# A decoder layer on one core: identity products in the front, an earlier first v, and the second gate and up ahead of P V

## What is computed

```python
x = x + attn(layernorm(x))            # sigmoid q, k; kv = k^T v per head; num/den; norm; gate; Wo; relu
x = x + xattn(layernorm(x), ctx)      # 16 heads of 64: softmax(q k^T / 8) v, then Wo + bo
x = x + ffn(layernorm(x))             # shared SwiGLU (256) + the SwiGLU of the expert that top-1 of 8 picks
```

## Time and profile before

| | us |
|---|---|
| median of 3 timed runs | 648.67 |
| lowest and highest | 648.15, 648.98 |
| the profiled execution | 643.3 |
| its span, first to last instruction | 641.6 |
| TensorE busy | 593.4 |
| VectorE busy | 428.0 |
| ScalarE busy | 424.9 |
| GpSimd busy | 310.7 |

### The profile page before, as it was taken

How to read it: one execution, slowest core, us unless ns; L and a number is a source line. 1 busy time by engine, 2 the same in 40 slices (tenths; PEclk the granted TensorE clock), 3 DMA queues, 4 the chain that set the end, 5 groups by cost and what they waited for, 6 DMA issues and landing times.

```text
span 641.6 us, 14968 instructions
## 1 busy us (share of the span) xinstructions
PE 593.4 (92%) x5231; PEld 514.1 (80%) x5231; DVE 428.0 (67%) x1185; ACT 424.9 (66%) x1512; POOL 310.7 (48%) x331
## 2 busy tenths in 40 slices
PE   3868999999999999999999999999999987999993
PEld 2767799889988998899989988998889876766661
DVE  3858665878685868586858685868564566376562
ACT  3538788777776787678677867786768764444551
POOL 3524644365336633663366336633652354147553
PEclk9969999999999999999999999999999998899997
DMA  7300000000010001000100000000000007325420
GB/s 161 98 18 13 17 2 2 13 18 2 2 30 18 17 3 30 18 18 2 30 18 17 1 15 17 17 2 2 17 18 1 2 27 227 115 72 157 144 74 8
DMA packets 24953, 23.49 MB, mean 37 GB/s; under 512 B 7007, under 2 KB 22497, under 8 KB 24880
## 3 DMA queue, kind: packets, MB, share of 16 engines
q1 hardware_dynamic: 20368, 14.91, 8.6%
q0 software_dynamic: 2784, 6.32, 2.7%
q10 hardware_dynamic: 1728, 1.32, 0.9%
HBM read 15.03 MB, written 7.95 MB: 36 GB/s over the span
## 4 chain that ended last, share of the span: by engine, by line
PE 70%; DVE 15%; ACT 7%; issue 3%; DMA 1%; POOL 1%; SPq 0%; DVEq 0%; POOLq 0%
PE bank L1128 9%; PE bank L1275 9%; PE bank L1243 8%; PE bank L1130 7%; PE bank L1129 7%; PE bank L1253 7%; PE bank L1264 5%; PE bank L1355 4%; ACT prob L1031 4%; PE bank L1224 2%; PE bank L1380 2%; PE bank L1135 2%; DVE stats L648 2%; DVE mneg L816 2%; ACT oT L1041 2%
## 5 line engine op out<-in xcount | busy, mean ns | idle before, releaser
L1031 ACT ACTIVATE prob<-bank,mneg 128x128 f32<-128x128 f32 x512 | 182.0, 376 | 80.1 <-DVE mneg L816 79.9
L560 POOL TENSOR_TENSOR prob<-prob,rden 128x512 f32<-128x512 f32 x128 | 130.7, 1041 | 107.1 <-DVE rden L823 106.8
L1031 ACT ACTIVATION_READ_ACCUMULATOR prob<-bank,mneg 128x1 f32 x512 | 109.8, 214 | 0.0
L1037 ACT COPY probT<-bank 128x512 f32<-128x512 f32 x128 | 76.8, 600 | 36.7 <-PE bank L1253 36.6
L816 DVE TENSOR_REDUCE mneg<-bank 128x4 f32<-128x512 f32 x128 | 80.3, 669 | 18.5 <-PE bank L1243 18.4
L1253 PE MATMUL bank<-ident,prob 128*128 128x128 f32 x512 | 78.4, 276 | 5.5 <-POOL prob L560 4.7
L499 POOL TENSOR_TENSOR rstd<-var_eps,neg_half 128x4 f32<-128x4 f32 x24 | 24.7, 1029 | 114.6 <-DVE var_eps L653 114.6
L1243 PE MATMUL bank<-kT,qT 64*128 64x128 f32 x1024 | 74.4, 285 | 2.9 <-issue 1.7
L1243 PEld LDWEIGHTS bank<-kT,qT 64*128 64x128 f32 x1024 | 62.2, 187 | 14.0 <-issue 11.4
L1253 PEld LDWEIGHTS bank<-ident,prob 128*128 128x128 f32 x512 | 60.6, 142 | 10.6 <-issue 6.2
L1264 PE MATMUL bank<-probT,V 128*64 128x128 f32 x1024 | 64.2, 279 | 0.0
(11 more groups left out here) (194 smaller groups left out, 1332.9 us busy)
## 6 DMA issues: line engine op xcount, KB each, us to landing
prob<-routed SPq DMA_DIRECT2D x39, 128.5 KB, 2.1
xin<-in_x_dram SPq DMA_DIRECT2D x8, 256.0 KB, 2.8
ctx_nat<-in_ctx_dram SPq DMA_DIRECT2D x8, 192.0 KB, 2.5
routed<-blank ACTq DMA_DIRECT2D x8, 128.5 KB
qT<-in_L_ffn_rt_gate_dram SPq DMA_DIRECT2D x1, 1024.0 KB, 5.9
qT<-in_L_ffn_rt_up_dram SPq DMA_DIRECT2D x1, 1024.0 KB, 11.1
out_dram<-probT,prob POOLq DMA_INDIRECT x39, 2.2
prob<-in_L_xattn_Wq_dram SPq DMA_DIRECT2D x1, 512.0 KB, 6.1
```

Of the source, the lines that this page charges most:

```text
L560: nc.gpsimd.tensor_tensor(view, view, spread(rden[:, m % 2, c * NC:(c + 1) * NC], 2, S), ALU.mult)\
L1031: last = nc.scalar.activation(prob[:, m % 2, p * S:(p + 1) * S], score_bank(m, c)[:, i * S:(i + 1) * S], ACT.Exp, bias=mneg[:, m % 2, p:p ...
L1037: nc.scalar.copy(probT[:, m % 2, c * 512:(c + 1) * 512], made(r1, ("T", m, c))[:])\
```

## The change

- The load of bq counts on a semaphore of its own. ScalarE's first casts wait for four loads, and the sigmoid of q for bq.
- TensorE multiplies the identity by itself 22 times at its start, as soon as the identity is there, and 8 times in slot (-4, 2) ahead of the turn of x1, into a bank of the scores that is unused then.
- Both halves of v of sequence 0 are made in slot (-4, 1), ahead of the last early piece of k, and emptied by ScalarE. They were made in (-1, 1) and (-1, 3) and emptied by VectorE. ScalarE's rounding of the cross-v weights goes from (-5, 3) to (-5, 2), VectorE's low part from (-4, 1) to (-5, 3), ahead of x1.
- The statistics of the second group of x go from (-5, 2) to behind those of x1, ahead of the normalisation of x1. GpSimd's rstd of them goes from (-5, 2) to (-4, 2).
- In the loop, "gate and up 1" is done ahead of P V in its slot, and "tanh 1" ahead of the copies of P V. VectorE's order stays.

```diff
--- before.py
+++ after.py
@@ -225,6 +225,7 @@
 
         w_in = sem("s1_weights_landed")
+        bq_in = sem("q_bias_landed")
         wx_in = [sem("cross_q_weights_landed"), sem("cross_k_weights_landed"), sem("cross_v_weights_landed")]
         wo_in = sem("output_weights_landed")
         xwo_in = sem("cross_output_weights_landed")
@@ -332,7 +333,7 @@
                  (NG - 2, "scatter 2"): (L6 + 2, 1), (NG - 2, "scatter 3"): (L6 + 2, 1),
                  (0, "turn context"): (-7, 2), (0, "context high"): (-7, 2), (0, "context low"): (-7, 2),
                  (0, "residual"): (-3, 0),
-                 (1, "stats of x"): (-5, 2), (1, "rstd of x"): (-5, 2), (1, "normalise x"): (-4, 3),
+                 (1, "stats of x"): None, (1, "rstd of x"): (-4, 2), (1, "normalise x"): (-4, 3),
                  (1, "turn x"): (-2, 3), (1, "copy x^T"): (-2, 3), (1, "x^T low"): (-2, 3),
                  (1, "project first pair"): (-1, 0), (1, "first pair"): (-1, 0),
                  (1, "project second pair"): (-1, 1), (1, "second pair"): (-1, 1)}
@@ -372,6 +373,12 @@
             pair = (n + 3) // 2 if n % 2 else (n + 2) // 2
             return early + [(part, pair, b)] * ((2 if part == "k" else 0) <= pair < B // 2)
+        def v_of(n, b):
+            if (n, b) == (-4, 1):
+                return [(0, 0), (0, 1)]
+            return [(n + 1, b // 2)] * (b % 2 and 0 < n + 1 < B)
         def qk_engine(part, pair, i):
             return "act" if i % 2 or (part == "k" and pair < 2) else "dve"
@@ -382,8 +389,8 @@
             for b in range(NC):
                 if live(n):
                     r1.add(("T", n, b), "act")
-                if b % 2 and live(n + 1):
-                    r1.add(("v", n + 1, b // 2), "dve")
+                for m, half in v_of(n, b):
+                    r1.add(("v", m, half), "dve" if m else "act")
                 for piece in qk_of(n, b):
                     r1.add(piece, qk_engine(*piece))
                 if b == 0 and live(n - 1):
@@ -391,12 +398,17 @@
                     r1.add(("PV", n - 1, 1), "act")
                 if b == 2 and live(n - 1):
                     r1.add(("out", n - 1), "dve")
+                for g, step in steps_at(PE_F, F_AT, n, b):
+                    if step == "gate and up 1":
+                        for u, engine in F_BANKS[step]:
+                            r2.add((g, u), engine)
                 for g, step in steps_at(PE_S1, S1_AT, n, b):
                     for u, engine in S1_BANKS[step]:
                         r2.add((g, u), engine)
                 for g, step in steps_at(PE_F, F_AT, n, b):
-                    for u, engine in F_BANKS[step]:
-                        r2.add((g, u), engine)
+                    if step != "gate and up 1":
+                        for u, engine in F_BANKS[step]:
+                            r2.add((g, u), engine)
         for step in itertools.chain.from_iterable(PE_TAIL.values()):
             for u, engine in F_BANKS[step]:
@@ -431,7 +443,7 @@
             sp.dma_start(rawkvh[:, D:2 * D], Wk).then_inc(w_in, 16)
             sp.dma_start(rawkvh[:, 2 * D:], Wv).then_inc(w_in, 16)
             sp.dma_start(rawq1, Wq).then_inc(w_in, 16)
-            sp.dma_start(bq_col[:], bq.rearrange("(p o) -> p o", o=1)).then_inc(w_in, 16)
+            sp.dma_start(bq_col[:], bq.rearrange("(p o) -> p o", o=1)).then_inc(bq_in, 16)
             load_ctx(0)
             sp.dma_start(rawk, XWk).then_inc(wx_in[0], 16)
             sp.dma_start(lnw_bc[:], bc(ln_w)).then_inc(wl_in, 16)
@@ -739,6 +751,8 @@
                     dve.wait_ge(x1_in, g + 1)
                     stats_of(2, x1)
                     if g == 0:
+                        s1(1, "stats of x")
                         normalise_first(x1n, x1, 2)
                 if step == "context low":
                     ps = made(r2, (g, 13))
@@ -915,8 +929,9 @@
                     if b % 2 == 0 and live(n + 1):
                         row_max(n + 1, b)
                         row_max(n + 1, b + 1)
-                    if b % 2 and live(n + 1):
-                        empty_v(n + 1, b // 2)
+                    for m, half in v_of(n, b):
+                        if m > 0:
+                            empty_v(m, half)
                     for piece in qk_of(n, b):
                         if qk_engine(*piece) == "dve":
                             empty_qk(*piece)
@@ -935,7 +950,7 @@
                         dve.wait_ge(wm_hi, 1)
                         nc.vector.tensor_tensor(sh_gu_lo[:], rawgu, sh_gu_hi[:].bitcast(F32), ALU.subtract)\
                             .then_inc(wm_lo, 1)
-                    if (n, b) == (FIRST + 3, 1):
+                    if (n, b) == (FIRST + 2, 3):
                         dve.wait_ge(w_hi, 3)
                         nc.vector.tensor_tensor(xwv_lo[:], rawv, xwv_hi[:].bitcast(F32), ALU.subtract)\
                             .then_inc(w_lo, 1)
@@ -1003,7 +1018,7 @@
                     nc.scalar.activation(hkv[:, :, D:2 * D], hkv[:, :, D:2 * D], ACT.Sigmoid).then_inc(k_sig, 1)
                     ps = made(r2, (g, 5))
                     if g == 0:
-                        act.wait_ge(w_in, 16 * 5)
+                        act.wait_ge(bq_in, 16)
                     nc.scalar.activation(qsT[:], ps[:], ACT.Sigmoid, bias=bq_col[:]).then_inc(r2.emptied["act"], 1)
                 if step == "copy gated^T":
                     nc.scalar.copy(gT[:], made(r2, (g, 10))[:]).then_inc(r2.emptied["act"], 1)
@@ -1041,6 +1056,10 @@
                 nc.scalar.copy(oT[:, m % 2, j * 512:(j + 1) * 512], made(r1, ("PV", m, j))[:])\
                     .then_inc(r1.emptied["act"], 1)
+            def empty_v(m, half):
+                nc.scalar.copy(V[:, m % 2, half * 512:(half + 1) * 512], made(r1, ("v", m, half))[:])\
+                    .then_inc(r1.emptied["act"], 1)
             def empty_qk(part, pair, i):
                 ps = made(r1, (part, pair, i))
                 dst = qT if part == "q" else kT
@@ -1060,7 +1079,7 @@
             act.dma_start(b_hkv[:, 2 * D:], bc(bv)).then_inc(wb_in, 16)
             act.dma_start(beta_bc[:], bc(beta)).then_inc(wb_in, 16)
-            act.wait_ge(w_in, 16 * 5)
+            act.wait_ge(w_in, 16 * 4)
             nc.scalar.copy(wkvh_hi[:], rawkvh)
             nc.scalar.copy(wq_hi[:], rawq1).then_inc(w1_hi, 1)
             for n in range(FIRST, B):
@@ -1072,9 +1091,15 @@
                         empty_T(n, b)
                     if live(n + 1):
                         exp_chunk(n + 1, b)
+                    for m, half in v_of(n, b):
+                        if m == 0:
+                            empty_v(m, half)
                     for piece in qk_of(n, b):
                         if qk_engine(*piece) == "act":
                             empty_qk(*piece)
+                    for g, step in steps_at(ACT_F, F_AT, n, b):
+                        if step == "tanh 1":
+                            ffn(g, step)
                     if b == 0 and live(n - 1):
                         empty_PV(n - 1, 0)
                         empty_PV(n - 1, 1)
@@ -1087,11 +1112,12 @@
                         act.wait_ge(wx_in[1], 16)
                         nc.scalar.mul(xwq_hi[:], rawq, DH ** -0.5).then_inc(w_hi, 1)
-                    if (n, b) == (FIRST + 2, 3):
+                    if (n, b) == (FIRST + 2, 2):
                         act.wait_ge(wx_in[2], 16)
                         nc.scalar.copy(xwv_hi[:], rawv).then_inc(w_hi, 1)
                     for g, step in steps_at(ACT_F, F_AT, n, b):
-                        ffn(g, step)
+                        if step != "tanh 1":
+                            ffn(g, step)
             for j in range(TILES + 3):
                 if j < TILES:
@@ -1300,21 +1326,33 @@
                 g, b = m // GB, m % GB
                 keys, cols = slice(b * S, (b + 1) * S), slice(half * 512, (half + 1) * 512)
                 if m == 0:
+                    pe.wait_ge(*r2.freed((g, 13)))
                     pe.wait_ge(w_lo, 3)
                 product3(ps[:], ctxT_hi[:, g % 2, keys], ctxT_lo[:, g % 2, keys], xwv_hi[:, cols], xwv_lo[:, cols])\
                     .then_inc(r1.ready, 1)
+            def stay_awake(count):
+                for _ in range(count):
+                    pe.matmul(bank[0][:, 0:P], ident[:], ident[:], start=True, stop=True)
             pe.wait_ge(consts, CONSTS_FIRST)
+            stay_awake(22)
             for n in range(FIRST, B):
                 for b in range(NC):
+                    if (n, b) == (-4, 2):
+                        stay_awake(8)
                     if live(n):
                         turn_probs(n, b)
                     if b % 2 == 0 and live(n + 1):
                         scores(n + 1, b // 2)
-                    if b % 2 and live(n + 1):
-                        make_v(n + 1, b // 2)
+                    for m, half in v_of(n, b):
+                        make_v(m, half)
                     for piece in qk_of(n, b):
```

(3 more changed lines are left out.)

## The result

| us | before | after |
|---|---|---|
| timed runs, first measurement, median (4 runs each) | 648.42 | 640.77 |
| lowest and highest | 648.15, 648.98 | 639.09, 641.09 |
| the profiled execution | 643.3 | 639.09 |
| its span | 641.6 | 637.4 |
| timed again, median | 643.03 (10 runs) | 635.65 (6 runs) |

The kernel after takes 0.9875 of the time before, 95% interval 0.986 to 0.9889: 7.65 us less, where 5.3 were forecast. (The 648.67 of the first part is the median of three of these four runs.)

A forecast was written before the change was run, and what follows sets the result against it. TensorE, busy 92%, was taken as the bound, losing time only in idle gaps and at low clock. Front -2.1 and loop -3.2 made -5.3 us: 638.0 profiled, plus 5.4 to the median, 643.4; range 640.5 to 647.0.

The forecast's parts named there:

- (6): Loop, seven times: gate ahead of P V and earlier tanh remove the waits of "down"; -3.2 us, between 0 and 4.1.
- (5): Slots (-1, 1) and (-1, 3): VectorE's second copy of V leaves the chain for ScalarE; -0.7 us.
- (2): Start: 22 identity products raise the clock for the context's turn; 0.2 us won, between 0.6 lost and 1.9 won.
- (3): Front: cross-v weights' parts ahead of x1 add 1.05 us, the second x's statistics 0.4.
- (4): Pause before x1's turn: identity and v products keep the clock high for q; first scores near 42.95, -1.4 us.
- (1): Start: bq on its own semaphore lets casts move earlier, but the context's DMA still holds the turn; 0 us.
- rival of the lost clock: Front: clock falls before q, front +0.5 us with the loop's gain kept; 646.0 us, chance 0.24.
- waits for probabilities might grow: End part near 540 us: sign of a wrong prediction if these waits grow by what the loop gave.
- The wait only moves: Loop: P V's bank is freed late and v takes over the 0.52 us; 646.6 or 649.2 us, chance 0.12.
- slower through ScalarE: Loop: ScalarE reaches tanh 1.1 us later, so v and k wait; 650.9 us down to 649.9, chance 0.10.
- Doesn't do what it says: Front: identity products don't count as work for the clock; treated as the lost-clock case, no separate chance.
- Both stages high: Front: the 22 products hold the clock through the projections, first scores 2.2 us earlier than forecast; 641.2 us, chance 0.20.

The follow-up runs named there:

- e1: Kernel before with the loop part alone (second gate and up ahead of P V, tanh ahead of its copies): 637.57 us, ratio 0.9912 to before.
- e2: Kernel after with the loop part taken back, leaving the front changes alone: 641.76 us, ratio 0.9973 to before.
- e5: Kernel after run once more without an edit: 635.65 us, ratio 0.9889 to before.
- e7: Kernel after without the 8 identity products ahead of the turn of x1, the 22 kept: 637.63 us, ratio 0.9915 to before.
- e12: Kernel before with the 22 and 8 identity products and nothing else: 642.63 us, ratio 0.9982 to before.
- e8: Kernel after with more identity products in the front's remaining pauses (26 at the start): 634.12 us, ratio 0.9852 to before.
- e11: Kernel after with v of sequence 0 and the cross-v weights' parts back in their old slots: 638.51 us, ratio 0.9921 to before.
- e4: Kernel before run once more, unchanged, for a second trace: 643.22 us, ratio 0.9995 to before.
- e9: Kernel before with only ScalarE's tanh moved ahead of the copies of P V, TensorE's order kept: 640.15 us, ratio 0.9943 to before.
- e10: Kernel before with only TensorE's second gate and up moved ahead of P V, ScalarE's order kept: 646.71 us, ratio 1.0047 to before.
- e6: Kernel after without the 22 identity products at the start, the 8 kept: 636.53 us, ratio 0.9896 to before.
- e3: Kernel after without any identity products, early v and the new order of statistics kept: 638.5 us, ratio 0.992 to before.

## Why the prediction was right and where it was wrong

The step that failed is term (6), the loop: the waits of "down" were counted at 0.42 us a group, by their printed idle less a loss at v, and 3.2 us in all. The runs showed 0.67 us a group, about 5.0 us in the seven places by the traces, and 5.7 us by e1's time. Term (5) failed too, -0.7 forecast and -0.07 measured, but errors in (2), (3) and (4) cancel it.

**(1) bq.** As forecast: ScalarE's first cast came 1.4 us earlier (9.41 for 10.81), and the turn of the context still waited for its DMA (0.89 us before 11.58). No run tries it alone.

**(2) The 22 products.** Forecast 0.2 us, between 0.6 lost and 1.9 won. The price and the end were right (44 records in 6.92 us, ending at 8.55), and so was the low clock at 12 to 16. What it then does scatters. The turn of gated, which ends this stage, came at 26.11, 25.61, 27.22, 27.66, 27.68, 27.26 and 27.60 in the seven traces with the 22 (after, e2, e5, e7, e12, e8, e11), mean 27.02; without them at 27.75, 27.54, 27.38, 28.21, 27.47, 27.53 and 28.50 (before, e4, e1, e9, e10, e6, e3), mean 27.77. So 0.75 us on average, and from 0.1 to 2.2 in one execution; with seven traces on each side, scattering over 2.1 and 1.1 us, the mean is uncertain by as much as its size. The two early ones, 25.61 and 26.11, are those in which the projections ran at 0.17 us, all of them in e2 and those from 15.9 us on in the first trace after. The Trainium skill ("TensorE: Matmul & The Clock Gate", Part 1) has the window run free of the kernel's start, so that the point of change differs between executions. The prediction said that no run showed it; the runs now do, in these traces, in the fall at 29.3 or 33 of the same kernel, and in the spread of the kernel before (641.65 to 645.22 in 20 runs).

**(3) The weights' parts ahead of x1.** Forecast +1.45 us (1.05 and 0.4); measured +1.0. From the turn of gated to the turn of x1 it takes 7.78 us in the trace before and 8.79, 8.78 and 8.80 in e7, e3 and e8, whose clock was high there. VectorE's timeline of the kernel after shows the order:

```profile
28.82 1.22 DVE L955 TENSOR_TENSOR xwv_lo<-prob,xwv_hi 96x1024 fp32r<-96x1024 f32 x1 [1.63 <-ACT xwv_hi L1117]
29.96 0.68 DVE L746 TENSOR_TENSOR x<-bank,bo_bc 128x512 f32<-128x512 f32 x1
...
32.80 0.86 DVE L660 BATCH_NORM_STATS2 stats<-xin 128x6 f32<-128x128 f32 x4
```

The second statistics fit almost wholly into the wait for the rstd: from x1's first step to the turn of x1 it takes 5.23 before and 5.39 here, 0.16 and not 0.4. The rest is VectorE's low part: x1's first step stands 2.55 us behind the turn of gated before and 3.40 in e7, 0.85 and not 1.05. (The forecast's own sum for this step gives 31.39, where it wrote 31.35.)

**(4) The eight products.** Right in size, and in mechanism with one exception: the clock was taken to stay up, and in three of the four traces it fell and rose again before q. The clock is high for q in all four traces that have the 22, the early v and the eight or more (after, e2, e5, e8); from the first q product to the first scores it takes 3.82 or 3.83 us there and 6.18 in the trace before, 2.35 won for 2.2 forecast. The first scores, forecast at 42.95 (-1.4), came at 42.82 in e5, 1.49 ahead of e4; in the first trace, with the early projections of (2), at 41.36. That 42.82 is so near is luck: in e5 x1 was turned about 0.8 us late behind the identity products, a cost that the forecast set at nothing, and (2) and (3) gave about as much back. The rival of the lost clock did not happen for q in these four, although the clock did fall earlier in after, e2 and e5; it was high again by 36 us after work nearly without a break. In e6 it did happen.

**(5) V off VectorE.** Forecast -0.7; measured -0.07. This step failed. From the first scores to those of four slots on (65.90 in the trace after, 68.95 before) it takes 24.60 or 24.61 us in e4, e11 and e12 and 24.54 in the kernel after, e5 and e6. The copy did leave the path, but what stood behind it, VectorE's low part of the gate weights, moved into GpSimd's products and took 1.46 us for 0.68. VectorE and GpSimd in the kernel after, then in e11 with the late copy:

```profile
49.99 1.46 DVE L951 TENSOR_TENSOR sh_gu_lo<-x,sh_gu_hi 128x512 fp32r<-128x512 f32 x1
...
48.84 2.06 POOL L572 TENSOR_TENSOR prob<-prob,rden 128x512 f32<-128x512 f32 x2
```

```profile
53.44 0.68 DVE L948 TENSOR_TENSOR sh_gu_lo<-x,sh_gu_hi 128x512 fp32r<-128x512 f32 x1
...
51.48 2.03 POOL L570 TENSOR_TENSOR prob<-prob,rden 128x512 f32<-128x512 f32 x2
```

With the copy in front, the step began at 53.44, as GpSimd ended at 53.51. Without it, it begins 1.15 us into GpSimd's two products and takes 0.78 us longer, as much as the copy's 0.69 gave. Every trace with the early v has it at 1.44 to 1.47 and every one without at 0.68; GpSimd's two products take 2.06 us for 2.03. In all seven with the early v it starts 0.13 to 0.15 us into GpSimd's second product and ends 0.55 us after that product, about as if it had stood still until then. It ends 10.12 us after the first scores in e5 and 10.18 in e11, and these 0.06 us are all that is left of the gain. The Trainium skill ("GPSIMD Engine Reference", Specifications) says that GpSimd shares its SBUF interfaces with VectorE and contends with VectorE's instructions that have two SBUF inputs; this step has two, and the trace agrees. Whether the 0.7 us comes back if the step is put elsewhere was not tried.

**(6) The loop.** Forecast -3.2 us (and the bound of all waits 4.1); measured -5.7. The mechanism was right: no wait of "down", a small loss at v (0.18 for 0.1), P V behind the gate, and the turn behind it within 0.11 us of its old distance. The size was wrong, because a printed idle is less than the wait costs. From the turn of probabilities near 131 us to the first scores near 479, with five of these waits between, it takes 348.05 us in the trace of before, 348.15 in e4 and 344.81 in e1: 0.65 to 0.67 us a group, where 0.52 were printed and 0.42 counted. One slot shows where they come from, in us from start to start:

| stretch, from the scores of slot (9, 0) to those of (9, 2) | e4 | e1 | less |
|---|---|---|---|
| first scores to the last k product ahead of P V or gate | 1.78 | 1.79 | -0.01 |
| to the turn of probabilities | 3.62 | 3.51 | 0.11 |
| to v | 0.35 | 0.53 | -0.18 |
| to the last k product ahead of "down" | 1.37 | 1.39 | -0.02 |
| to "down" | 0.81 | 0.12 | 0.69 |
| to the next turn | 1.86 | 1.78 | 0.08 |
| to the next scores | 0.53 | 0.53 | 0 |
| together | 10.32 | 9.65 | 0.67 |

The rows of e4, and the turn behind "down" in e1:

```profile
195.31 0.28 PE L1130 MATMUL bank<-ctxT_hi,xwk_lo 96*128 96x256 f32 x1
196.12 2.02 PE L1224 MATMUL bank<-sh_dn,act 128*128 128x128 f32 x16 [0.53 <-DVE act L787]
197.98 0.60 PE L1253 MATMUL bank<-ident,prob 128*128 128x128 f32 x4
```

```profile
196.89 0.60 PE L1262 MATMUL bank<-ident,prob 128*128 128x128 f32 x4
```

The idle is printed from the end of the last k product, 0.28 us after its start, but in a stream the next product starts 0.12 after it. So the wait costs 0.69 us for the 0.53 printed, and 0.08 more because "down" takes longer from a standstill. The two waits of 0.75 in the end part gave 0.82 and 0.85 (from the scores at 479 us to the routing's count at 522 it takes 42.72 us in e4 and 41.90 in e1, from there to the turn of probabilities at 539 16.99 and 16.14), where 0.6 was counted. That makes 3.3 + 1.7 = 5.0 us, well inside e1's interval.

The 0.7 us between this and e1's 5.7 has no cause that is shown. The two traces do differ by it in the stretch from the turn of probabilities at 538.88 in the trace before to the gate products at 562.45: before, e2, e4 and e12 take 23.2 to 23.6 us for it, and e1, e3, e5 and e6 22.5 to 22.6, e8 21.9. But after, e7 and e11 take 23.1, 23.6 and 23.5 with the loop part too, e9 takes 22.7, and e10, the slowest kernel of all, 22.3. So it may be scatter of that stretch, which holds a wait of 2.9 us for probabilities and a low clock in every trace. The warning that waits for probabilities might grow by what the loop gave did not come true: 4.6 us for 4.7.

**The rivals.** "The wait only moves" and "slower through ScalarE" fell: ScalarE was at tanh at 192.47, 0.40 ahead of the 192.87 of the earlier trace rows as the whole slot is (187.77 for 188.19), and not 1.1 us late. e10 shows that this order can be slower, 3.0 us, by another mechanism: tanh left behind the copies. "Doesn't do what it says" fell with e7. The 649.9 us for the mild end of the slower case follows from no sum there: its own lag of 0.9 us gives 0.8 us over the median, 649.5. "Both stages high" and the forecast are the same kernel on different executions, and not rivals: I gave chances to what is in truth a spread within each measurement.

**The move to the median.** The sum was made at the profiled execution, 643.3, and moved up by 5.4. In the later measurements the kernel before has medians of 643.0 to 643.8. So the 5.4 us were not a difference between a profiled and a timed execution of this kernel, but belonged to the first timing, whose ratio agrees with the later one all the same. Its cause is open.

The sum again, with what was measured. Front: -2.1 forecast, 0.55 more by (2), 0.45 more by (3), 0.15 more by (4), 0.63 less by (5): -2.6 by the traces, without the 0.8 us that the identity products cost in e2 and e5; e2 measured -1.7, with an interval from -0.6 to -2.8. Loop: -3.2 forecast, -5.7 by e1. Together -7.4 by the two kernels for the -5.3 of the forecast. That the front came out near its forecast is luck, errors that cancel; the loop missed by its one.

## What to carry to other kernels

A wait on the bounding engine is worth more than its printed idle: measure it as the distance between the same step in two slots, with and without the wait (0.67 us for a printed 0.52 here). When two orders on two engines are changed together, price each alone: here one brings 3.7 us, the other costs 3.0, and both bring 5.7. When a stretch is filled to hold the clock, look whether the filler ends before the work that it waits with: at the low clock the eight products cost 0.8 us of what they won. A step that leaves an engine's path lets the next one start earlier, and beside other company: look at what the other engines do at its new time before the gain is booked.

## What the runs showed of the hardware

- VectorE's subtraction of two 128 x 512 fp32 operands in SBUF took 0.68 us where it met only the last 0.07 us of a product of GpSimd, and 1.44 to 1.47 where GpSimd's multiplication in SBUF (1.04 to 1.06) began 0.13 to 0.15 before it.
- TensorE's clock fell about the pause before the turn of gated (1.60 to 1.73 us), inside it or up to 1.8 us behind it, in the traces of after, e1, e2, e4, e5, e6, e11 and e12, and stayed high through the same pause in those of before, e3, e7, e9 and e10. Idle fp32 products of the identity, 0.12 us a record, placed in the pauses, kept it at 1.00 from 20 to 44 us in e8.
- In the first trace after, and in no other, the routed tail stopped once: TensorE 2.40 us and ScalarE 2.59, with a low clock behind it. The same stretch has no such pause in e5. It took 4 us of that execution; its cause is open.

```profile
578.98 0.69 PE L1410 MATMUL bank<-ident,V 128*128 128x128 f32 x2 [2.40 <-issue]
...
577.63 0.38 ACT L1130 ACTIVATE oT<-bank 128x256 f32<-128x256 f32 x1 [2.59 <-PE bank L1394]
```
